# Orthogonal convolution by block elimination over 580 frequencies: larger sets, updates in halves, pivots gathered unit by unit, and a last solver stage pipelined over pairs

## The reference

```
xfft = rfft2(pad(gn(x)))                      # 34 x 18 frequencies
vfft = rfft2(weight, s=(34, 34))              # per frequency a 128 x 127 complex matrix V
wfft = conj(V).T @ V + eps * I
W    = I - 2 V wfft^-1 conj(V).T
out  = x + irfft2(W @ xfft)[inner 32 x 32] + bias
```

## Time and profile before

| | us |
|---|---|
| median of 3 runs (lowest, highest) | 4109.44 (4084.66, 4148.07) |
| the profiled execution's own time | 4130.5 |
| its span | 4128.3 |

### The profile page before, as it was taken

The page is one execution under the profiler, slowest core; times in us unless marked ns, Lnnn a source line. Parts: engine busy times, 40 slices in busy tenths (PEclk is TensorE's granted clock), DMA queues, the critical chain, the costliest instruction groups (busy, mean ns, idle before and its releaser), DMA issues. The chain is left out here.

```text
span 4128.3 us, 97147 instructions
## 1 busy us (share of the span) xinstructions
PE 2959.8 (72%) x42317; PEld 2379.4 (58%) x42317; DVE 2165.5 (52%) x4711; ACT 1163.9 (28%) x2659; POOL 716.1 (17%) x1331
## 2 busy tenths in 40 slices
PE   6875376332988888888877877866697666647677
PEld 3375334222776666667666665655576555547677
DVE  4184327777786667765687576566504672002122
ACT  1332122111443443443423232212243222211111
POOL 2400000000221122211223223111222222200000
PEclk6597788666998999987877576556797566657667
DMA  5443501000222123211311112010232011232332
GB/s 164 80 94 70 92 27 24 1 1 1 56 49 45 41 54 68 41 37 44 69 48 48 34 41 68 25 32 28 54 78 61 28 51 49 71 95 103 110 118 85
DMA packets 286453, 235.84 MB, mean 57 GB/s; under 512 B 216696, under 2 KB 228600, under 8 KB 285192
## 3 DMA queue, kind: packets, MB, share of 16 engines
q1 hardware_dynamic: 254784, 146.84, 14.9%
q0 software_dynamic: 31248, 82.79, 7.0%
HBM read 126.15 MB, written 103.28 MB: 56 GB/s over the span
## 5 line engine op out<-in xcount | busy, mean ns | idle before, releaser
L1274 DVE SCALAR_TENSOR_TENSOR arena<-arena,psum 128x448 f32<-128x448 f32 (+1 forms) x640 | 403.6, 693 | 673.3 <-PE psum L910 673.3
L1238 DVE TENSOR_TENSOR arena<-arena 128x192 f32<-128x192 f32 (+7 forms) x720 | 456.6, 634 | 24.8
L889 PEld LDWEIGHTS psum<-arena 32*32 32x32 f32 x9280 | 186.0, 132 | 466.0 <-issue 459.1
L889 PE MATMUL psum<-arena 32*32 32x64 f32 x9280 | 216.5, 257 | 327.6 <-issue 220.8
L910 PE MATMUL psum<-arena 32*128 32x64 f32 x9280 | 360.8, 310 | 93.7 <-DVE arena L1274 92.8
L910 PEld LDWEIGHTS psum<-arena 32*128 32x128 f32 x9280 | 339.2, 223 | 135.2 <-issue 116.1
L1233 DVE TENSOR_TENSOR arena<-arena 128x960 f32<-128x960 f32 (+2 forms) x600 | 408.4, 714 | 12.4
L777 POOL COPY arena<-arena 128x464 f32<-128x464 f32 x160 | 85.6, 581 | 1580.1 <-ACT arena L1076 1580.1
L1371 PE MATMUL psum<-arena 68*128 68x64 f32 x1152 | 184.6, 338 | 185.2 <-DMA arena<-yhat 125.0
L1371 PEld LDWEIGHTS psum<-arena 68*128 68x128 f32 x1152 | 181.2, 252 | 186.8 <-DMA arena<-yhat 126.1
L858 PE MATMUL psum<-arena 128*32 128x256 f32 (+1 forms) x1744 | 186.6, 492 | 119.9 <-DMA arena<-plain 90.2
(11 more groups left out here) (125 smaller groups left out, 5584.4 us busy)
## 6 DMA issues: line engine op xcount, KB each, us to landing
kept<-arena POOLq DMA_DIRECT2D x145, 256.0 KB, 2.8
arena<-kept SPq DMA_DIRECT2D x145, 256.0 KB, 2.9
xhat<-arena SPq DMA_DIRECT2D x32, 580.0 KB, 13.0
yhat<-arena POOLq DMA_DIRECT2D x290, 64.0 KB, 2.4
arena<-yhat SPq DMA_DIRECT2D x64, 272.0 KB
arena<-x SPq DMA_DIRECT2D x8, 2048.0 KB, 9.6
arena<-x SPq DMA_DIRECT2D x32, 512.0 KB, 14.9
out<-arena POOLq DMA_DIRECT2D x32, 512.0 KB, 6.3
```

The costliest lines, as they stand in the source:

```text
L889: ins = pe.matmul(psum[0][h, L * t:L * t + L], ce[h, sj % NCE, slot + t, :], M[h, home(q) + t, c, :], start=True, stop=True)
L1238: link(dve.tensor_tensor(rest, rest, pr[:, :, h], op))
L1274: ins = dve.scalar_tensor_tensor(old, old, K["mask"][:, piv:piv + 1], psum[2 + c][:, 0:L * n].rearrange("p (t n) -> p t n", n=L), ALU.mult ...
```

## The change

- **Sets.** The sets hold 32, 32, 32, 32 and 17 quads in place of five times 29. Groups a and b have 64 quads each, in units of 8; group c has 17, in units of 6, 6 and 5. `M` holds 128 quads. To make room, `bx`, `x2_in`, `x_turned` and `ys` share memory with `part_in` and `work`, and `dt` has one buffer; mids and finals wait for each other where they now share memory.
- **Update in halves.** A unit's update is two halves of two classes each. Half h uses banks 2 + 2 (h mod 3) and the next, so three halves are in flight over six banks, and TensorE waits for VectorE's half h - 3.
- **Gather.** ScalarE gathers the pivots of a unit, four copies of 32 partitions by 128 elements, one unit behind the sweep.
- **Final.** `part_in`, `q_emb` and `x_turned` have four buffers. TensorE turns the next pair between `solve_z` and `sum_y` of this one. `copy_beside` moves from GpSimd to ScalarE.

```diff
-SLOTS, QUAD = 29, 4
+QUAD = 4
+FIRST = [0, 32, 64, 96, 128, NQ]
-UNITS_OF_SET = [8, 7, 7, 7]
+UNITS_OF_SET = [[8] * 4] * 4 + [[6, 6, 5]]
...
-        dt = a(2, 2, B, SP_)
+        dt = a(2, B, SP_)
...
+        def upd_bank(half, c):
+            return psum[2 + 2 * (half % 3) + c % 2]
...
                     def load_part(m):
-                        if m >= 2:
-                            sp.wait_ge(S["y_done"], m - 1)
+                        if m >= 4:
+                            sp.wait_ge(S["y_done"], m - 3)
...
                         elif kind == "mid":
+                            if before("final", at):
+                                sp.wait_ge(S["y_done"], before("final", at))
...
                         elif kind == "final":
+                            sp.wait_ge(S["s_done"], before("mid", at))
...
                     def update(u):
                         pe.wait_ge(S["ju_copied"], u + 1)
-                        if u:
-                            pe.wait_ge(S["upd_copied"], u)
-                        for t in range(n):
-                            for c in range(QUAD):
-                                rows = u_emb[quadrant(cls(p, c)), u % 2, t]
-                                ins = pe.matmul(psum[2 + c][:, L * t:L * t + L], rows.rearrange("p q r m -> p (q r m)"),
-                                                real_half(rows), start=t == 0, stop=t == n - 1)
-                        ins.then_inc(S["upd_done"], 1)
+                        for half in (2 * u, 2 * u + 1):
+                            if half >= 3:
+                                pe.wait_ge(S["upd_copied"], half - 2)
+                            for t in range(n):
+                                for c in (2 * (half % 2), 2 * (half % 2) + 1):
+                                    rows = u_emb[quadrant(cls(p, c)), u % 2, t]
+                                    ins = pe.matmul(upd_bank(half, c)[:, L * t:L * t + L], rows.rearrange("p q r m -> p (q r m)"),
+                                                    real_half(rows), start=t == 0, stop=t == n - 1)
+                            ins.then_inc(S["upd_done"], 1)
...
+                    def gather_next(g, k, u):
+                        q, n, _, sj = sweep_units[u]
+                        act.wait_ge(S["upd_copied"], 2 * u + 2)
+                        gather(set_job_at[g, k + 1, set_jobs[sj][2]], q, n)
```

More of the change, by code:

```diff
@@ L707, in build @@
                  "q_turned", "q_copied", "q_beside", "jq_copied", "z_done", "z_copied", "y_done", "y_copied"]
-        for n in ("bx_in", "x2_in", "part_stored", "part_in", "y_stored"):
+        for n in ("bx_in", "x2_in", "part_stored", "y_stored"):
             names += [n + "0", n + "1"]
+        names += [f"part_in{n}" for n in range(4)]
         with ExitStack() as es:
@@ L821, in _ @@
                         elif kind == "mid":
-                            pool.wait_ge(S["upd_copied"], swept(g, LB - 1))
+                            pool.wait_ge(S["upd_copied"], 2 * swept(g, LB - 1))
                             if before("final", at):
                                 pool.wait_ge(S["y_done"], before("final", at))
+                                for n in range(2):
+                                    pool.wait_ge(S[f"y_stored{n}"], 32 * len(final_quads[n:before("final", at):2]))
                             for m in range(lo, hi):
@@ L1049, in _ @@
                             settle(j)
[L1050 to L1057 removed]
+                            pairs = [range(m, min(m + 2, hi)) for m in range(lo, hi, 2)]
+                            for m in pairs[0]:
+                                turn_q(m)
+                            for n, two in enumerate(pairs):
+                                for m in two:
+                                    solve_z(m)
+                                for m in pairs[n + 1] if n + 1 < len(pairs) else ():
+                                    turn_q(m)
+                                for m in two:
+                                    sum_y(m)
                 @block.scalar
@@ L1160, in _ @@
                             copy_ju(lo)
-                            done = {set_jobs[set_job_at[g, k, t]][3]: t for t in GROUPS[g]}
                             for u in range(lo, hi):
@@ L1165, in _ @@
                                     copy_ju(u + 1)
-                                for end in (u, u + 1) if u + 1 == hi else (u,):
-                                    if end in done and k % LB != LB - 1:
-                                        act.wait_ge(S["upd_copied"], end)
-                                        gather(set_job_at[g, k + 1, done[end]])
+                                if k % LB != LB - 1:
+                                    if u > lo:
+                                        gather_next(g, k, u - 1)
+                                    if u + 1 == hi:
+                                        gather_next(g, k, u)
                         elif kind == "mid":
+                            if before("final", at):
+                                for n in range(2):
+                                    act.wait_ge(S[f"y_stored{n}"], 32 * len(final_quads[n:before("final", at):2]))
                             copy_b(lo)
```

180 lines of the change are left out of this document (86 added, 94 removed).

## The result

The changed kernel takes 4237.25 us (median of 4 runs, 4228.62 to 4241.42), the kernel before, run beside it, 4100.27 us. The ratio is 1.034, with a 95% interval of 1.030 to 1.039. The forecast was 3833 us and its range ended at 3945. The profiled execution took 4228.62 us, with a span of 4226.7 us and a mean granted clock of 0.73.

A forecast was written before the change was run, and what follows sets the result against it. TensorE and VectorE taking turns bound full-clock sweeps; the factor, or finals waiting for `kept`, bound other stages. Terms 12 - 19 + 41 - 60 - 153 - 97 = -276 us gave a median of 3833 us, range 3740 to 3945.

The forecast's parts named there:

- B's sweeps: Eight sweeps in the stage of mids beside factors: 42.5 us each, 340 in all, for 369.0 before.
- A's sweeps: Sweeps a 0 to 3, the first stage after the forms: 167 us for 179.0 before.
- B's mids and the rest of B: Mids beside factors, in the stage with eight sweeps: 12 more quads add 70 us, 758 in all.
- C's sweeps: Sweeps b 4 to 7, each behind an idle TensorE, half of them staying at half clock: 214 us for 207.6.
- C's gaps: Finals a beside factors, between sweeps b 4 to 7: 275 us for 341.9, with 2.8 us per quad.
- D's sweeps: Group c's eight sweeps, now 17 quads in three units at half clock: 19.7 us each, 157 for 224.3.
- the rest of D: Finals b, group c's gaps and its mid: gaps -16 us, twelve quads fewer in the mid -67; 491 in all.
- E: Final c, the last solver stage: 17 quads at 2.8 us each, 52 us for 148.5.
- Rival 4: Clock stays at half in every sweep of 8 units and every final: 4213 us, chance 0.03.
- Rival 1: Finals don't get faster, the four-deep buffers finding another wait: 3949 us; chance 0.13.
- rival 2: In sweeps, a small gather on ScalarE costs 0.98 us like a large one: 3924 us; chance 0.12.
- rival 3: The clock is full soon in every sweep: 3632 us; chance 0.05.

The follow-up runs named there:

- e1_joint: The changed kernel with an update's matmuls issued over all four classes again, banks and two signals kept; 3744.91 us, 0.908 of the kernel before.
- e6_joint_nooverlap: As e1_joint, but an update waits until VectorE has subtracted the whole unit before; 3856.4 us, 0.936 of the kernel before.
- e2_before_two: The kernel before with an update's matmuls in two pairs of classes, same banks and waits; 4412.46 us against 4124.68, one run.
- e7_joint_oldfinal: As e1_joint, but the final's turn, solve and sum in the order of before, four buffers kept; 3728.58 us, 0.9045 of the kernel before.

## Why the prediction was wrong

**The step that failed** is the one in the sweeps: "With three halves in flight VectorE's 2.73 us per unit are hidden beside TensorE's 4.04". VectorE's time is hidden, as said. But the 4.04 was summed from an update of 1.94 us that the rows show for four classes in turn, and the change issues them two by two. I priced the update by its count of matmuls and a duration from a row, and didn't ask whether the duration of one still held in the new order. The order of instructions that stands with the change shows the two runs in place of one, and I read past it. At full clock the sum is 3.33 + 1.06 + 1.03 = 5.4 us a unit for the 4.15 predicted; at half clock it is 845.59 - 835.49 = 10.10 for the 7.55. With the order undone the 4.04 itself comes out (4.03 in e1_joint, and 7.49 at half clock), so TensorE's other terms were right. One reading beside it was low: the prediction has "some 4.7" for the cycle before, where rows 2 have 1127.90 - 1122.95 = 4.95 us for an update of 8 quads, and e6_joint_nooverlap has 4.91. It made the overlap look smaller than it is and has nothing to do with the loss.

**The clock made it worse.** Of the 128 updates of 8 quads, 58 lay wholly at half clock in the kernel after, 35 partly and 35 not at all. In e1_joint those were 7, 10 and 111. In the sweeps of A, B and C the two kernels differ by 473 us (1088 against 615). With nine updates in ten at full clock, as in e1_joint, the lost concurrency alone would be 128 x (0.9 x 1.39 + 0.1 x 2.61) = 194 us, from the 1.94 and 3.33 us of an update at full clock and the 3.62 and 6.23 at half. The other 280 us are what is left, and most of it is the clock by this estimate: 51 more updates wholly at half clock, each of whose units is 10.10 - 5.4 = 4.7 us longer, are 240 us. That the clock follows from the order is shown by e2_before_two, in which only the order was changed and the clock in B's sweeps went from 0.86 to 0.70 (one run), and by e1_joint, in which it went from 0.74 to 0.96. Why the chip grants less to it was not settled.

**Stage by stage**, the sweeps by the windows above:

| term | forecast, us | measured | miss |
|---|---|---|---|
| forms | 145 | 138 | -7 |
| A's sweeps | 167 | 306 | +139 |
| A, three gaps | 195 | 196 | +1 |
| B's sweeps | 340 | 499 | +159 |
| B's mids and the rest of B | 758 | 737 | -21 |
| C's sweeps | 214 | 306 | +92 |
| C's gaps | 275 | 277 | +2 |
| D's sweeps | 157 | 175 | +18 |
| the rest of D | 491 | 479 | -12 |
| E | 52 | 50.5 | -1.5 |

The misses in the sweeps add up to 408 us, and all the others to -39. So every other step came out well: the gap of D (47.5 us for 49), a gather of 128 elements (1.64 to 1.66 us for four, 0.41 each, for 0.40), final c (50.5 us for 52), and the new waits of shared memory, of which no stage shows a cost.

**The finals** got faster by the step named (no more waits of 2 us a pair for `kept`: 0.22 and 0.18 in the rows above, 2.15 in rows 7). But e7_joint_oldfinal shows that the reordering, which I had taken for a part of the gain, has none in it.

**Rival 4** named a clock that stays at half in sweeps and finals, 4213 us, with a chance of 0.03, and 4237 came out. That its size is near is luck. Its point of decision held (a mean cycle above 6.3 us; from update to update it is 7.9 in the sweeps of A to C, and 4.3 in e1_joint). Its mechanism did not: the finals and mids kept their clock (final c 0.96), most of the price was paid in sweeps, and in those both clocks cost more than it had. Rival 1, rival 2 and rival 3 did not come about. **The chances** were at fault too. The forecast, rivals 1 and 2 and the range rested on one cycle at full clock, and its parts were read from rows of another order. The 0.94 for faster was in truth the chance of that one step, for which the trace of before had no row. The prediction had said that a cycle above 4.6 us at full clock would show it wrong, and the cycle is 5.4.

## What to carry to other kernels

When work is split in two so that one engine can run ahead of another, look at what the split does to the engine that was already busy. The small matmuls of these kernels ran side by side as far as they stood in different row groups. So keep every row group at work in each stretch of such an update. In e1_joint the halves still have banks and signals of their own, but the order goes round all four classes and both signals come at the end; this kept the overlap (4.03 us a unit) and cost nothing. A duration from a row holds for instructions in the neighbourhood in which they stood there, and a reordering is a change of that neighbourhood.

The best version measured is the change with the update issued over all four classes and the final's order of before: 3728.58 us, 9.6% under the kernel before (ratio 0.9045, 0.900 to 0.909). With the final's order of the change it is the same within the noise (0.908).

## What the runs showed of the hardware

- Matmuls of 32 rows, 128 stationary and 64 moving columns in f32, each with a load of its own, start 27.7 ns apart at full clock when they go round four row groups and 49.8 ns apart on two; at half clock 52, 93.5 and, on one, 171 to 176 ns. Whether two or four banks are written and whether VectorE reads beside them changes this by less than 2 ns.
- TensorE busy for 75.06 of 77.90 us had a granted clock of 0.54 (two row groups). In e6_joint_nooverlap, where TensorE goes round four row groups and stands idle for 0.8 us of each 4.9, B's sweeps had 0.91, for the 0.74 of the kernel after, whose units have no idle time. The Trainium skill (TensorE: Matmul & The Clock Gate, "Why this matters for your kernels") has it that a TensorE kept busy without gaps gets the full clock. Here being busy was not enough, and the measurement decides. What in the two-class order lowers the clock these runs don't tell.
- A small cost in an in-order queue grows: 2.54 us idle in the middle of a sweep, 2.7 us more at its end and a lower clock (0.85 for 0.96) came with the gather of whole sets, 125 us together where I had expected at most 20.

Not tried: a half made of four quads with all four classes, spread over banks of its own, so that VectorE can start in the middle of an update. With the signals at the end VectorE is hidden already, so little is left for it at full clock.
